# A selective scan with a mixture of experts beside it: the experts' gate by one activation with its own table

## The reference

```
h[n]   = h[n] * exp(dt * A[n]) + (dt * x) * B[n]      for n in 16 states, along time
y      = sum over n of h[n] * C[n]
expert = silu(x @ gate) * (x @ up) * weight            for 32 experts of width 64
out    = sum over experts of expert @ down
```

## Time and profile before

| | |
|---|---|
| time, median of 3 runs | 6929.41 us (6923.68 to 6935.76) |
| the profiled execution: its own time | 6921.02 us |
| its span from the first to the last instruction | 6919.2 us |
| mean granted clock of TensorE, as a share of full speed | 0.864 |
| busy over the whole span | PE 5147.8, DVE 5178.2, ACT 4138.5, POOL 1827.9 us |
| the scan stage | about 340 to 1125 us of the span |

### The profile page before, as it was taken

The page is one execution under the profiler, slowest core; times in us unless marked ns, Lnnn a source line. Parts: engine busy times, 40 slices in busy tenths (PEclk is TensorE's granted clock), DMA queues, the critical chain, the costliest instruction groups (busy, mean ns, idle before and its releaser), DMA issues. The chain is left out here.

```text
span 6919.2 us, 84441 instructions
## 1 busy us (share of the span) xinstructions
PE 5147.8 (74%) x23563; PEld 1831.3 (26%) x23563; DVE 5178.2 (75%) x6483; ACT 4138.5 (60%) x5955; POOL 1827.9 (26%) x1241
## 2 busy tenths in 40 slices
PE   4499987879548778332333688888867999999999
PEld 2133332333212222000000122222214444444443
DVE  5399996343667664697896699999974888888887
ACT  3466664424445446798896699999971333333333
POOL 0077773000010000000000000000001777777776
PEclk7699998879779889555555799999996999999999
DMA  0000000000032130000001233332331101111110
GB/s 18 26 1 0 0 0 18 15 0 0 17 107 40 21 64 14 15 0 14 0 0 37 58 44 39 44 40 40 45 37 34 27 20 31 31 25 23 31 31 13
DMA packets 205415, 176.97 MB, mean 26 GB/s; under 512 B 145523, under 2 KB 186751, under 8 KB 196831
## 3 DMA queue, kind: packets, MB, share of 16 engines
q1 hardware_dynamic: 205038, 172.33, 13.0%
HBM read 121.05 MB, written 51.23 MB: 25 GB/s over the span
## 5 line engine op out<-in xcount | busy, mean ns | idle before, releaser
L2076 DVE TENSOR_REDUCE cs_neg<-cs_s_ps 128x1 f32<-128x1024 f32 x1024 | 1185.0, 1215 | 67.1 <-PE cs_s_ps L1940 49.1
L1994 ACT ACTIVATE cs_E<-cs_s_ps,cs_neg 128x1024 f32<-128x1024 f32 x1024 | 1136.6, 1115 | 69.1 <-DVE cs_neg L2076 61.5
L2349 ACT ACTIVATE da_P<-da_P 128x1024 f32<-128x1024 f32 x512 | 541.2, 1057 | 931.4 <-DVE da_P L2424 912.4
L2390 POOL TENSOR_TENSOR da_psum<-da_psum,da_P 128x1024 f32<-128x1024 f32 x384 | 904.9, 2356 | 367.2 <-ACT da_P L2349 334.3
L2407 DVE TENSOR_REDUCE da_mx<-da_s_ps 128x1 f32<-128x1024 f32 x512 | 623.8, 1220 | 199.3 <-PE da_s_ps L2273 199.2
L1368 PE MATMUL hypb_o_ps<-hypb_P,hypb_vq 128*32 128x512 f32 (+3 forms) x640 | 193.6, 932 | 608.6 <-DVEq L1758 404.6
L2424 DVE TENSOR_TENSOR da_P<-da_s_ps,da_lift 128x1024 f32<-128x1024 f32 x512 | 600.6, 1215 | 3.5 <-PE da_s_ps L2277 3.4
L1940 PE MATMUL cs_s_ps<-cs_q,cs_k 64*128 64x512 bf16 x2048 | 401.9, 396 | 261.4 <-ACT cs_E L1994 220.5
L2273 PE MATMUL da_s_ps<-da_k,da_q 64*128 64x512 f32 x2048 | 552.3, 617 | 22.3 <-DMA da_v<-vf 16.2
L1951 PE MATMUL cs_r_ps<-cs_E,cs_w 128*32 128x512 f32 x4096 | 550.8, 612 | 2.5 <-POOL cs_w L2036 0.9
L568 POOL TENSOR_TENSOR scan_hC<-scan_h,scan_c_sb 128x512 f32<-128x512 f32 x256 | 400.2, 1583 | 559.7 <-DVE scan_h L605 558.3
(11 more groups left out here) (448 smaller groups left out, 9294.1 us busy)
## 6 DMA issues: line engine op xcount, KB each, us to landing
da_q<-qf SPq DMA_DIRECT2D x32, 512.0 KB, 8.8
da_k<-kf SPq DMA_DIRECT2D x32, 512.0 KB, 10.5
cs_q<-q_parts SPq DMA_DIRECT2D x384, 32.0 KB
cs_k<-k_parts SPq DMA_DIRECT2D x384, 32.0 KB
qf<-cs_side_sb SPq DMA_DIRECT2D x32, 256.0 KB, 3.5
kf<-cs_side_sb SPq DMA_DIRECT2D x32, 256.0 KB, 5.3
vf<-cs_side_sb SPq DMA_DIRECT2D x32, 256.0 KB, 5.7
da_v<-vf SPq DMA_DIRECT2D x16, 512.0 KB, 11.6
```

Of the source, the lines that this page charges most:

```text
L1994: act.activation(E[:, seg.slot(t, E_RING), h, :], s_ps[:, seg.slot(u, RING, 2), :], ACT.Exp, bias=neg[:, g, j, h:h + 1], accum_out=z[:, g, ...
L2076: dve.tensor_reduce(neg[:, g, j, h:h + 1], s_ps[:, seg.slot(u, RING, 2), :], AX.X, ALU.max, negate=True).then_inc(maxed, 1)
L2349: act.activation(P[:, g % RING, :, :], P[:, g % RING, :, :], ACT.Exp).then_inc(exped, 1)
L2390: pool.tensor_tensor(psum[:, :, :], psum[:, :, :], P[:, g % RING, :, :], ALU.add).then_inc(pooled, 1)
```

## The change

The gate of the experts is made by one activation, Silu, straight from g_ps. The three other activations of `sigmoid`, the tile sig and the product on POOL go. Silu lies in another table than Exp, so each step now holds two loads of a table: the load is put in by the compiler ahead of the activation that needs it. PE's `gate`, which used to wait until g_ps had been read twice (gate_taken), waits for the Silu of the block before (silu_done); DVE's `times_up`, which waits for silu_done too, now gets it from ACT and not from POOL. The single load ahead of the stage goes.

```
-        dtx, gate_sb, sig, hid = (scratch[...] for i in range(4))
+        dtx, gate_sb, hid = (scratch[...] for i in range(3))
...
                 def gate(g, n):
-                    wait(pe, gate_taken, blk(g, n) * 2 + 2)
+                    if known(g, n, 1):
+                        wait(pe, silu_done, blk(g, n))
...
             def _(act):
-                act.sem_inc(gate_taken, 2)
-                act.preload_act_table_set("natural_log_exp_and_others")
...
                 def sigmoid(g, n):
                     wait(act, gate_ready, blk(g, n) + 1)
                     wait(act, hid_done, blk(g, n) + 1)
-                    act.activation(sig[:, n % 2, :], g_ps[:, :], ACT.Exp, scale=-1.0).then_inc(gate_taken, 1)
-                    act.activation(gate_sb[:, n % 2, :], g_ps[:, :], ACT.Copy).then_inc(gate_taken, 1)
-                    wait(act, gate_taken, blk(g, n) * 2 + 4)
-                    act.activation(sig[:, n % 2, :], sig[:, n % 2, :], ACT.Ln, bias=1.0).then_inc(logged, 1)
-                    wait(act, logged, blk(g, n) + 1)
-                    act.activation(sig[:, n % 2, :], sig[:, n % 2, :], ACT.Exp, scale=-1.0).then_inc(sig_done, 1)
+                    act.activation(gate_sb[:, n % 2, :], g_ps[:, :], ACT.Silu).then_inc(silu_done, 1)
...
-                def silu(g, n):
-                    lasting(sig_done, blk(g, n) + 1)
-                    pool.tensor_tensor(gate_sb[:, n % 2, :], gate_sb[:, n % 2, :], sig[:, n % 2, :], ALU.mult).then_inc(silu_done, 1)
...
                     for n in range(NE):
                         weigh(g, n)
-                        if known(g, n, 1):
-                            silu(*at(g, n, 1))
```

More of the change, by code:

```diff
@@ L437, in scan_with_experts @@
         h, hC = sc.sb("h", [128, 2, CH]), sc.sb("hC", [128, 2, CH])
-        dtx, gate_sb, sig, hid = (scratch[:, 2 * i * CH:2 * (i + 1) * CH].rearrange("p (k c) -> p k c", c=CH) for i in range(4))
+        dtx, gate_sb, hid = (scratch[:, 2 * i * CH:2 * (i + 1) * CH].rearrange("p (k c) -> p k c", c=CH) for i in range(3))
         carry = sc.sb("carry", [128, 2 * D_STATE])
@@ L445, in scan_with_experts @@
         hc_ready, hc_used, dtx_done, y_taken, gated = (sc.sem(n) for n in ("hc_ready", "hc_used", "dtx_done", "y_taken", "gated"))
-        gate_ready, gate_taken, logged, sig_done = (sc.sem(n) for n in ("gate_ready", "gate_taken", "logged", "sig_done"))
+        gate_ready = sc.sem("gate_ready")
         silu_done, factors_ready, up_done, hid_done = (sc.sem(n) for n in ("silu_done", "factors_ready", "up_done", "hid_done"))
@@ L582, in _ @@
                     emit(g)
-                silu(LAST, NE - 1)
             @block.vector
```

## The result

The change made the kernel faster by about 1.2%: the median is 6850.11 us (4 executions, 6846.24 to 6853.55) against 6932.59 for the kernel before on the same chip (4 executions), ratio 0.9881, interval 0.9864 to 0.9898. A second measurement gave 6845.37 us against 6927.02, ratio 0.9874 (0.9858 to 0.9891). That is some 82 us less, where 63 were forecast; 6850 lies inside the range that was given.

What follows compares the result with a forecast made beforehand. DVE was taken to bound the scan stage, its scans lengthened by POOL's gate product. 100 steps x (5.79 - 5.18) = -61 us, dtx -5, the other 28 steps +3: -63, so 6866 us against the median, range 6834 to 6902.

Steps and rivals of the forecast that it cites:

- The product on POOL goes: Scan stage: 100 first scans lose 0.86 us each, 85.9 us of excess, and DVE's step falls to 4.93 us.
- Loads without hidden cost: ACT in each step: a table load costs its row of about 1.28 us, with the next activation 0.01 us behind.
- The slower rival: ACT's loads hide 1.19 us each, making its step 7.56 us and the kernel 7112 us; chance 0.09.
- ACT becomes the pace, at 5.18 us: Scan stage: with two loads ACT's step is 5.13 to 5.23 us, just above DVE's 4.93.
- the rival in which ACT is not the pace: Scan stage: DVE gets all its 86 us and 7 of dtx, -93, 6836 us; chance 0.13 for DVE or PE as pace.
- About half a us to spare: ACT's copy to c_sb, and its Exp steps: each has about half a us before it must wait.
- PE's new wait costs nothing as long as ACT is the pace: PE's gate product waits for the previous block's Silu; PE is 0.5 us or so early, so no cost.
- dtx -5: DVE's dtx products, which also meet POOL, 14 us in all: a gain of 5 us, with 0 and 14 as ends.
- the other 28 steps ... +3: Steps at segment heads, already without the meeting: about half held to ACT's pace by a quarter us, +3 us.
- 100 x 0.61: Scan stage: 100 of 128 steps shorten from 5.79 to 5.18 us, -61 us together.
- the scan meeting: POOL's gate product lies over DVE's first scan, lengthening the scan pair from 2.45 to 3.31 us in about 100 steps.

Runs made afterwards that it cites:

- e6: The kernel after with a POOL product of two different tiles put back in each step: 6929.41 us, ratio 1.0001 to the kernel before.
- e2: The kernel before with only its POOL gate product taken out, the four activations kept: 6838.74 us, ratio 0.9865 to the kernel before.
- e7: The kernel after with two POOL fills of a spare tile, which read nothing, in each step: 6849.82 us, ratio 0.9883 to the kernel before.
- e4: The kernel after with a third, useless table load ahead of the Silu in each step: 6968.68 us, ratio 1.0052 to the kernel before.
- e3: The kernel after with Exp in place of Silu for the gate, so no table loads in the steps: 6828.82 us, ratio 0.9859 to the kernel before.
- e1: The kernel after with a POOL product reading one spare tile twice put back in each step: 6893.68 us, ratio 0.9944 to the kernel before.

## Why the prediction was right, and where its size was off

- **The product on POOL goes: right.** The mechanism is shown by e6, e2 and e7. Its amount was counted low: 85.9 us were predicted for the scans and the means give 90.7. The prediction set the shortest scans, one by one, against the busy time of groups in which the two scans of a pair overlap a little, and so lost some 5 us.
- **Loads without hidden cost: right**, by e4 and by the gaps in ACT's timeline. The slower rival (7112 us) is out.
- **ACT becomes the pace, at 5.18 us: right in kind, its price far too high.** Steps last 5.04 or 5.18 in the middle of a segment, ACT busy for 29.61 of 30 us there. The pair of Exp took 1.33 where 1.42 was read. The prediction let ACT cost 5.18 - 4.93 = 0.25 us a step; by e3 it costs 5.09 - 5.03 = 0.06, since the steps with ACT at the limit are shorter than 5.18 on average and those without loads longer than 4.93: PE and DVE stand right behind. So the rival in which ACT is not the pace (6836 us) came nearer to the measured time than the forecast (6866), and its terms, all of DVE's meetings in the scans and 7 us of dtx, are what DVE gained. In its mechanism e4 speaks against it: an engine with room would have hidden part of the third load, and of its 1.29 us only 0.05 were hidden.
- **"About half a us to spare" at the copy to c_sb: wrong.** The hC pair that began at 566.09 and lasted 3.14 us ended at 569.23, and the copy began at 569.33:

```profile
566.09 3.14 POOL L561 TENSOR_TENSOR scan_hC<-scan_h,scan_c_sb 128x512 f32<-128x512 f32 x2 [2.03 <-DVE scan_h L591]
```

  0.1 us is what lay between them in the other steps that I read as well. What had been counted wrong is the start of the load for Exp: 1.3 us or more behind the end of the first scan, where it came 566.68 - 565.75 = 0.93 behind (the first of the two scans below ends at 565.75), and the Exp pair was shorter too. ACT and POOL arrive at the copy together. It cost little, as ACT was busy until 569.30.

```profile
564.47 2.45 DVE L591 TENSOR_TENSOR_SCAN scan_h<-scan_dA,scan_carry,scan_dBx 128x512 f32<-128x512 f32 x2
```

- **PE's new wait costs nothing as long as ACT is the pace: right, though PE does stand.** Over most of the stage (440 to 1050 us) PE's queue waited for the Silu 98 times, 58.7 us in all:

```profile
PEld scan_g_ps L487 <- ACT x L538: 58.7, 98, 1.0
```

  DVE's idle ahead of line 601 is where this chain can reach it: 15.3 us in the stage, and 8.6 of that kind stood ahead of line 615 in the kernel before, which the prediction had taken for zero:

```profile
L615 DVE TENSOR_TENSOR x<-x,scan_u_ps 128x512 f32<-128x512 f32 x128 | 86.1, 673 | 8.6 <-PE scan_w_ps L491 8.6
```

  The condition was not needed: e3 has the new wait and an ACT with room, e2 the old one, and their segments are equally long (259.4 and 259.5 us for three and a product).

- **The term that was mis-sized: "dtx -5" and "the other 28 steps ... +3", -2 us together.** In the middle steps the sum came out by luck: 11 a segment, 88 in all, went from 5.77 to 5.09 on average (steps of 5.04 and 5.18), 88 x 0.68 = 60 us, against the 61 predicted as 100 x 0.61. Too many steps and too little for each are two errors that cancel. The heads gave the rest, some 21 us. From the first dBx of the last step to that of the next segment it was 633.52 - 624.24 = 9.28 us (the dBx pair begins 1.20 before the scan of 625.44) and is 601.13 - 593.79 = 7.34: the scan meeting goes there too, and the dtx pair falls from 3.24 to 2.17 us. The step after it goes from 641.78 - 633.52 = 8.26 to 608.68 - 601.13 = 7.55; 0.34 of that are products of `take_output` that read two tiles of SBUF and met POOL's product too, a term that the prediction did not have. Before, then after:

```profile
640.23 1.63 DVE L630 TENSOR_TENSOR mamba_xs<-mamba_xs,mamba_zs  x2
```

```profile
607.47 1.29 DVE L616 TENSOR_TENSOR mamba_xs<-mamba_xs,mamba_zs  x2
```

  The two steps together give 1.94 + 0.71 = 2.65 us a segment at this head, 8 x 2.65 = 21 us. At the heads DVE has its own work and sets the pace alone, ACT waits for it, and so each us that DVE loses there counts in full. The prediction charged its meetings at the heads to ACT's pace, and took 5 of dtx's 14 us, where DVE's busy time for it fell from 24.0 to 16.5, by 7.5.

So the direction and the mechanism were right, and the sum for the middle of the segments came out by two errors that cancel; the 19 us by which the gain was undersized are the heads.

## What to carry to other kernels

When an engine's identical instructions have two durations, line up the other engine that reads the same memory with them: here a product that nobody waited for cost 0.86 us a step on the bound engine, and taking it over into an activation that ACT had room for won nearly all of it (91.9 us of DVE's time, of which 10.0 came back as idle). Look at which of the two begins first: here the later one waited. Three engines that end within a few per cent of one another left room for about one such move: two loads a step cost 7 us in all, a third 123. Size the heads of segments apart from the steps in between: where the bound engine works alone, a saving counts in full.

## What the runs showed that I had not expected

- A POOL product of 128 x 512 f32 that reads one tile twice takes 1.04 us, with two tiles 1.27 (e1 and e6).
- The scan's loss follows the overlap, not a fixed price: 0.84 us of overlap cost 0.64 (e1), 1.07 (657.98 + 1.28 - 658.19) cost 0.87 (e6), so all but the first 0.2 us. 0.63 us of overlap with fills cost nothing (e7).
- 253 table loads, 325 us of ACT's time, moved the end by about 7 us, because ACT had been idle for 784.60 - 533.52 = 251 us of the stage and lost three activations a step besides.
